# A four-layer graph network on one core: the row gathers written out without index copies and bounds, the attention sums' one-hots moved from VectorE to ScalarE

## The chip, the cores and the metric

The kernel runs on one core of one Trainium2 chip. The metric is the time of one execution on the device in microseconds. The kernel before was timed twice: 10643.65 and 10651.53 us, median 10647.59 us.

## What is computed

A graph of 6250 nodes (256 features each) and 100,000 edges, which are sorted by their destination. Each of four layers normalizes the node rows (layernorm, then max with 0), runs a graph layer over the edges and adds the result to the node rows:

```
edge_index = jnp.stack([src, dst])
h = jnp.maximum(_layernorm(x), 0.0); x = x + _L0_gnn_ref(h, ...)    # attention, 4 heads, feed-forward, 2 batch norms
h = jnp.maximum(_layernorm(x), 0.0); x = x + _L1_gnn_ref(h, ...)    # weighted sums over edges, both directions
h = jnp.maximum(_layernorm(x), 0.0); x = x + _L2_gnn_ref(h, ...)    # two rounds of plain sums: segment_sum(h[src], dst)
h = jnp.maximum(_layernorm(x), 0.0); x = x + _L3_gnn_ref(h, ...)    # attention, 8 heads
```

In layer 0 the weight of an edge is `exp(att . leaky(xl[src] + xr[dst]))` over its sum by destination, in layer 3 it comes from `s_u[src] + s_v[dst]` in the same way. What all layers share is the gather of table rows by `src` and the sum of edge rows by `dst` (`segment_sum`).

## The kernel before

**Edges as tiles.** The edges are padded to 784 tiles of 128 edges, one edge to a partition. Two tiles are a pair (392 pairs), 128 nodes are a node tile (49). A visit is a pair of edge tiles that meets one node tile: there are 440 visits, so 880 steps (one edge tile in one visit). A unit is four visits, so eight steps: there are 110 units. For every step the setup has put the position of each edge's destination inside the node tile into a column of `rel`, and the source node of every edge into `gidx`, one column for each edge tile.

**A sum by destination** is a matmul: for each step a 128x128 one-hot matrix (`iota == rel` column, edge on the partition, node on the free axis) is the stationary side and the edge rows are the moving side; TensorE adds the two steps of a visit up in a PSUM bank (four banks), and VectorE adds the bank to the node tile in SBUF (`add_visits`, line 956).

**A gather** is an indirect DMA that GpSimd issues (`gather`, line 1005): one for each edge tile, 128 rows of 256 to 264 floats by the 128 indices of one column. Five passes make 784 of them each:

- `attention_fetch0` (layer 0), into `regionB`: the gathered row and the destination's row (by matmul) are added, leaked (line 1378), transposed and multiplied by the attention vector, and the gathered rows are stored in DRAM (`Eb`) in the order of the edges
- `plain_pass` 'l1' (layer 1), into `rows_in`: weighted one-hots tile by tile (line 944), sums by destination, and a fold of sums of the other direction (line 1174)
- `plain_pass` 'l2a' and 'l2b' (layer 2), into `rows_in`: plain one-hots, one instruction for the eight steps of a unit (`one_hots`, line 941)
- `attention_fetch3` (layer 3), into `regionC`: the scores of the edges are added up and the rows are stored in `Eb`

The slots of the gathered rows are a ring of groups (four gathers to a group, in `attention_fetch3` eight). SyncE counts a group as landed and gives its slot back when the visits that read it are done (`landed_groups`, line 967). GpSimd's own loop is: wait for the slot (line 1010), copy the index columns of the next groups from `gidx` to a small tile `gather_rows` (`index_columns`, line 1000; four columns at a time in `attention_fetch0`, else eight) and wait for that copy (line 1002), then four or eight gathers (line 1014) with a bounds check against the table's last row. The loop's body is written out for one turn of the ring or two (48 to 32 gathers) and run over and over.

**The attention sums** (`attention_sum`, line 1405, for layer 0 as 'a0' and for layer 3 as 'a3') read the edge rows back from `Eb` in a plain DMA. For each unit VectorE does, in this order: the eight one-hots in one instruction (line 941), four multiplications of a pair's rows by their weights (line 1498), and then the four additions to the node tiles of the unit before (line 956). ScalarE waits until VectorE has done with the slot (`slot_kept`, line 1440) and copies the columns beside the 256 features (line 1444): logits, and in 'a0' also peaks and last marks, so 12 copies for a unit in 'a0' and 4 in 'a3'. TensorE (line 1466) waits for the one-hots, for ScalarE's columns (`lhs_full`), for each multiplication, and for the addition that frees its bank.

All waits are semaphores written out by hand; each engine's order of work is the order of its code. No planner is in between.

## Time and profile before

| | |
|---|---|
| time, 2 runs | 10643.65 to 10651.53 us, median 10647.59 |
| span of the profiled execution | 10655.6 us |
| TensorE matmul busy | 6231.9 us (58%) |
| VectorE busy | 5016.8 us (47%) |
| GpSimd busy | 5743.0 us (54%) |
| ScalarE busy | 1330.7 us (12%) |
| mean granted TensorE clock | 0.738 of full speed |
| bytes moved by DMA | 1358.92 MB, mean 128 GB/s |

The profile holds one execution: for each instruction its engine, start, duration and what it waited for. No time of that execution is given beside its span, which is 8 us above the median of the two runs (0.08%). The page's sum of shares is an average over stages that have different limits: GpSimd is busy in the five gather passes and idle in the attention sums, VectorE the other way round. So the rows below are taken stage by stage.

### The profile page before, as it was taken

Reading aid. Unit: us, or ns where it says so; the run is one execution under the profiler, and the core shown is the slowest. Engines: PE = TensorE matmul, PEld = TensorE weight load, DVE = VectorE, ACT = ScalarE, POOL = GpSimd, SP = SyncE. Lnnn points to the kernel's source line nnn. Section 1 sums busy time; section 2 is a strip of 40 time slices with the busy share of each in tenths; the row PEclk is TensorE's granted clock in tenths of the full one; section 3 lists DMA queues with packets and bytes.
Section 4 is the critical chain, followed back from the end, with each engine's and each line's share of the span. In section 5 each row is a group of like instructions: output and inputs, shape, how many; then the busy total and the mean of one; then the engine's idle time right before and its main releaser. Section 6 shows DMA issues by size and latency. Waiting matters only on the chain. (4 is left out here: it accounts for less than half of the span.)

```text
span 10655.6 us, 136733 instructions
## 1 busy us (share of the span) xinstructions
PE 6231.9 (58%) x24674; PEld 4869.8 (46%) x24675; DVE 5016.8 (47%) x12212; ACT 1330.7 (12%) x3940; POOL 5743.0 (54%) x5511
## 2 busy tenths in 40 slices
PE   4888975766466666555554665656665633222575
PEld 2888864545344444433333444444444433222454
DVE  6555558885444444355553222342222411115888
ACT  2122211213222222200001000010000300000000
POOL 3777740000188888866665777747776156762000
PEclk9898888888777777766666777777777655555798
DMA  4666665541277777744443333323332256662454
GB/s 147 188 189 188 187 214 167 168 148 43 57 104 105 104 105 104 99 137 136 133 129 93 88 88 89 88 79 88 88 87 85 69 178 199 198 191 85 134 169 154
DMA packets 835067, 1358.92 MB, mean 128 GB/s; under 512 B 112278, under 2 KB 488660, under 8 KB 834980
## 3 DMA queue, kind: packets, MB, share of 16 engines
q0 software_dynamic: 315328, 634.04, 27.0%
q1 hardware_dynamic: 385684, 562.46, 16.2%
q10 hardware_dynamic: 133968, 161.50, 4.9%
q8 instruction: 26, 0.43, 0.0%
q14 instruction: 61, 0.50, 0.0%
HBM read 943.05 MB, written 414.50 MB: 127 GB/s over the span
## 5 line engine op out<-in xcount | busy, mean ns | idle before, releaser
L1014 POOL DMA_INDIRECT rows_in<-table,gather_rows x2352 | 2470.6, 1050 | 944.0 <-issue 693.5
L1105 PE MATMUL ps_p<-rows_in,hot 128*128 x5280 | 1916.0, 524 | 1518.2 <-issue 527.6
L1105 PEld LDWEIGHTS ps_p<-rows_in,hot 128*128 128x128 f32 x5280 | 1312.6, 262 | 2081.5 <-issue 1850.3
L1724 POOL DMA_INDIRECT scatter_sums<-regionC,idx x880 | 1386.4, 1575 | 305.7 <-issue 245.1
L956 DVE TENSOR_TENSOR regionC<-regionC,ps_p 128x257 f32 (+2 forms) x1320 | 558.9, 423 | 1566.4 <-DVEq L953 1080.8
L1466 PE MATMUL ps_p<-regionA 128*128 128x265 f32 (+1 forms) x3520 | 964.9, 433 | 432.6 <-DVE regionB L956 199.3
L1466 PEld LDWEIGHTS ps_p<-regionA 128*128 128x128 f32 x3520 | 732.5, 213 | 664.6 <-DVE regionB L956 244.8
L1014 POOL DMA_INDIRECT regionB<-table,gather_rows x784 | 846.1, 1079 | 344.5 <-issue 293.9
L1014 POOL DMA_INDIRECT regionC<-table,gather_rows x784 | 813.0, 1037 | 297.3 <-issue 265.4
L1929 PE MATMUL psS<-dst_scores,regionA 128*128 x1760 | 393.3, 362 | 852.1 <-issue 427.1
L1929 PEld LDWEIGHTS psS<-dst_scores,regionA 128*128 128x128 f32 x1760 | 383.5, 330 | 861.9 <-issue 861.9
L1797 PE MATMUL psC<-regionC 128*128 128x128 f32 x1760 | 370.4, 377 | 653.6 <-PEq L1795 652.1
L1809 PE MATMUL psO<-regionA,regionC 128*128 x1760 | 666.0, 546 | 9.8 <-PEq L1808 2.8
L1797 PEld LDWEIGHTS psC<-regionC 128*128 128x128 f32 x1760 | 318.7, 271 | 757.9 <-issue 757.9
L956 DVE TENSOR_TENSOR regionB<-regionB,ps_p 128x265 f32 (+1 forms) x880 | 373.2, 424 | 506.3 <-DVEq L953 264.0
L1539 POOL MEMSET ones<- 128x128 f32 x2 | 0.4, 204 | 1122.8 <-POOLq L2054 954.3
L1319 PEld LDWEIGHTS psL<-att_cols,featT 128*128 128x128 f32 x3520 | 519.8, 213 | 61.9 <-issue 31.2
L1498 DVE TENSOR_TENSOR regionA<-regionA,logits 128x512 f32<-128x512 f32 x880 | 547.9, 685 | 0.0
L1809 PEld LDWEIGHTS psO<-regionA,regionC 128*128 128x128 f32 x1760 | 488.9, 292 | 119.5 <-issue 24.5
L1294 PE MATMUL psX<-regionA,regionB 128*128 x1760 | 526.6, 428 | 26.8 <-PEq L1290 20.5
L1371 DVE TENSOR_TENSOR feat<-regionB,psX 128x512 f32<-128x512 f32 x440 | 302.1, 687 | 507.2 <-DVEq L1370 357.7
L1319 PE MATMUL psL<-att_cols,featT 128*128 128x4 f32 x3520 | 471.4, 257 | 16.6 <-PEq L1312 8.3
(303 smaller groups left out, 7671.2 us busy)
## 6 DMA issues: line engine op xcount, KB each, us to landing
regionA<-edge_rows SPq DMA_DIRECT2D x880, 256.0 KB, 3.3
edge_rows<-regionB SPq DMA_DIRECT2D x196, 512.0 KB
edge_rows<-regionC SPq DMA_DIRECT2D x392, 256.0 KB
regionC<-srcrow_d SPq DMA_DIRECT2D x220, 256.0 KB
scatter_sums<-zero_rows ACTq DMA_DIRECT2D x8, 6400.0 KB, 42.2
regionA<-scatter_sums ACTq DMA_DIRECT2D x49, 1024.0 KB
rows_in<-table,gather_rows POOLq DMA_INDIRECT x2352
regionB<-rrow_d ACTq DMA_DIRECT2D x110, 256.0 KB
```

Source lines behind the costliest of these rows:

```text
L956: v.tensor_tensor(dst_, dst_, ps[(u.c * VG + j) % nbank][:, 0:width], ALU.add).then_inc(s_add.sem, 1)
L1014: g.indirect_dma_start(out=rows_of(b * per + j), out_offset=None, in_=table, in_offset=bass.IndirectOffsetOnAxis(ap=rows[j], axis=0), boun ...
L1105: x = te.matmul(ps[(u.c * VG + j) % NB][:, 0:width], hot[:, b, 2 * j + k, :], at_tile(G, slot[j] * 2 + k), start=k == 0, stop=k == 1)
L1294: x = te.matmul(psX[b][:, k * D:(k + 1) * D], spread[:, ub, at:at + P], at_tile(A256, nt), start=True, stop=True)
L1319: x = te.matmul(psL[gb][:, col:col + HEADS0], featT[:, b, 2 * k + c, :], attc[:, c, :], start=c == 0, stop=c == 1)
L1371: v.tensor_tensor(feat[:, b, :], G[:, bass.ds(slot * 2, 2), :].rearrange('p a c -> p (a c)'), psX[b][:, :], ALU.add).then_inc(own_v, 1)
L1466: x = te.matmul(ps[(u.c * VG + j) % NB][:, 0:width], hot[:, b, 2 * j + k, :], Gs[:, b * GS + 2 * j + k, :], start=k == 0, stop=k == 1)
L1498: v.tensor_tensor(o, i, w, ALU.mult).then_inc(aux_full[b], 1)
L1724: g.indirect_dma_start(out=scat, out_offset=bass.IndirectOffsetOnAxis(ap=idx[:, b, j:j + 1], axis=0), in_=sums[:, b, j, :], in_offset=None ...
L1797: x = te.matmul(psC[b][:, j * P:(j + 1) * P], hot[:, b * Q + j, :], same[:, b * Q + j, :], start=True, stop=True)
L1809: x = te.matmul(psO[2 * b + j // 2][:, j % 2 * D:(j % 2 + 1) * D], pairs[:, b * Q + j, :], at_tile(SUP, nt[j // 2]), start=True, stop=True)
L1929: x = te.matmul(psS[b][:, j * HEADS3:(j + 1) * HEADS3], spread[:, b, j * P:(j + 1) * P], at_tile(SV, nt[j // 2]), start=True, stop=True)
```

## The change

Three things, and small ones beside them:

- `gather` has no loop any more: all 784 gathers of a pass are written out, each with its own fixed column of `gidx` as the index, so that the copy to `gather_rows` and the wait for it are gone, and the bounds check too.
- In `attention_sum` VectorE no longer makes the one-hots. ScalarE does, after its wait for the slot and before its copies: eight activations `Square(iota - rel)` of 128x128 with a column of `minus` (= -rel) as bias, a wait for them, and one `Relu(1 - x)` over the 128x1024 of the unit. Peaks and last marks lie in one table of five columns, so that 'a0' has 8 copies for a unit instead of 12.
- In 'l2a' and 'l2b' the plain one-hots are made by eight `tensor_scalar` of 128x128 instead of one `tensor_tensor` of 128x1024.
- Beside these: the group number in the waits of TensorE (line 1102) and VectorE (line 1368) is masked with 255, and SyncE reads one number with `value_load`.

```
@@ -909,13 +909,13 @@
                         v.sem_inc(res_free[b], 1)
-                    if last is not None:
+                    if peak is not None:
                         for c in range(SB):
                             v.sem_inc(res_full[b], -1)
-                            v.tensor_copy(peak[:, c * P:(c + 1) * P, :], ps[b][:, 0:512].rearrange('p (h s) -> p s h', s=P))
-                            v.tensor_copy(last[:, c * P:(c + 1) * P], psE[b][:, 0:P]).then_inc(own_v, 1)
+                            v.tensor_copy(peak[:, c * P:(c + 1) * P, 0:H], ps[b][:, 0:512].rearrange('p (h s) -> p s h', s=P))
+                            v.tensor_copy(peak[:, c * P:(c + 1) * P, H], psE[b][:, 0:P]).then_inc(own_v, 1)
                             v.wait_ge(own_v, 1)
@@ -936,9 +936,8 @@
                     x.then_inc(hot_full[0], 1)
-def one_hots(v, hot, u):
-    shape = [P, GS, P]
-    return v.tensor_tensor(hot, iota[:, :].unsqueeze(1).to_broadcast(shape), rel[:, bass.ds(u.val * GS, GS)].unsqueeze(2).to_broadcast(shape), ALU.is_equal)
+def one_hot(v, hot, s):
+    return v.tensor_scalar(hot, iota[:, :], rel[:, bass.ds(s, 1)], None, ALU.is_equal)
 def weighted_one_hot(v, hot, s, wgt):
@@ -966,7 +965,6 @@
     behind = ring // 2
-    regs = registers(sp, 'by_visit', 1)
     def group(u):
@@ -977,7 +975,7 @@
         b = u.c % ring
-        done = of_visits(sp, visits_by[0:1, :], u.val, regs, NV)[0]
+        done = sp.value_load(visits_by[0:1, bass.ds(u.val, 1)], min_val=1, max_val=NV)
         if kept:
@@ -993,34 +991,20 @@
         sp.sem_inc(ring_free[b], -1)
-def index_columns(g, u, ring, per, idx, together):
-    b, at = (u.c % (together * ring), u.c % together)
-    if at == 0:
-        n = together * per if not isinstance(u.val, int) else min(together * per, ET - u.val * per)
-        g.tensor_copy(idx[:, b * per:b * per + n], gidx[:, bass.ds(u.val * per, n)]).then_inc(own_p, 1)
-        g.wait_ge(own_p, 1)
-        g.sem_inc(own_p, -1)
-    return [idx[:, b * per + j:b * per + j + 1] for j in range(per)]
-
-def gather(g, table, rows_of, s_rows, ring, per, free, idx, together):
-    top_row = g.to_reg(NP - 1)
-
-    def fetch(u):
-        b = u.c % ring
+def gather(g, table, rows_of, s_rows, ring, per, free):
+    for n in range(ET // per):
+        b = n % ring
         g.wait_ge(free[b], 1)
         g.sem_inc(free[b], -1)
-        rows = index_columns(g, u, ring, per, idx, together)
         for j in range(per):
-            g.indirect_dma_start(out=rows_of(b * per + j), out_offset=None, in_=table, in_offset=bass.IndirectOffsetOnAxis(ap=rows[j], axis=0), bounds_check=top_row, oob_is_err=True).then_inc(s_rows[b].sem, 16)
-    for t_ in turns(g, ET // per, together * ring, 0):
-        fetch(t_.at(0))
+            column = n * per + j
+            g.indirect_dma_start(out=rows_of(b * per + j), out_offset=None, in_=table, in_offset=bass.IndirectOffsetOnAxis(ap=gidx[:, column:column + 1], axis=0)).then_inc(s_rows[b].sem, 16)
 def plain_pass(name, table, acc, acc_flat, width, weighted, fold=None, own=None):
         G = sb('rows_in', [P, RG * EG, width], F32, ctx)
-        idx = sb('gather_rows', [P, 2 * RG * EG], I32, ctx)
         hot = sb('hot', [P, 2, GS, P], F32, ctx)
@@ -1086,7 +1070,7 @@
             def _(g):
-                gather(g, table, lambda k: G[:, k, 0:D], s_rows, RG, EG, ring_free, idx, 2)
+                gather(g, table, lambda k: G[:, k, 0:D], s_rows, RG, EG, ring_free)
             @block.tensor
@@ -1099,7 +1083,7 @@
                     for j in range(VG):
-                        te.wait_ge(s_landed.sem, group[j] + s_landed.base)
+                        te.wait_ge(s_landed.sem, (group[j] & 255) + s_landed.base)
                         te.wait_ge(s_add.sem, u.val * VG + (j + 1) + s_add.base)
@@ -1155,7 +1139,8 @@
                     else:
-                        x = one_hots(v, hot[:, b], u)
+                        for j in range(GS):
+                            x = one_hot(v, hot[:, b, j, :], u.val * GS + j)
                     x.then_inc(hot_full[b], 1)
@@ -1255,7 +1239,7 @@
             def _(g):
-                gather(g, T0, lambda k: G[:, k, :], s_rows, RG0, EG, ring_free, idx, 1)
+                gather(g, T0, lambda k: G[:, k, :], s_rows, RG0, EG, ring_free)
             @block.scalar
@@ -1365,7 +1349,7 @@
                     group = v.snap(groups[u.c % VG], min_val=0, max_val=NEG)
-                    v.wait_ge(s_landed.sem, group + s_landed.base)
+                    v.wait_ge(s_landed.sem, (group & 255) + s_landed.base)
                     v.wait_ge(res_full[b], 1)
@@ -1412,6 +1396,7 @@
     with ExitStack() as ctx:
+        minus = sb('minus_rel', [P, S], F32, ctx)
         ps = [bank(f'ps_p{i}', ctx) for i in range(NB)]
@@ -1438,6 +1423,12 @@
                     a.sem_inc(slot_kept[b], -1)
+                    for j in range(GS):
+                        x = a.activation(hot[:, b, j, :], iota[:, :], ACT.Square, bias=minus[:, bass.ds(u.val * GS + j, 1)])
+                    x.then_inc(own_a, 1)
+                    a.wait_ge(own_a, 1)
+                    a.sem_inc(own_a, -1)
+                    a.activation(hot[:, b].rearrange('p s e -> p (s e)'), hot[:, b].rearrange('p s e -> p (s e)'), ACT.Relu, bias=1.0, scale=-1.0).then_inc(hot_full[b], 1)
                     for j in range(VG):
@@ -1474,6 +1465,9 @@
                     v.sem_inc(back_free[b], 1)
+                v.tensor_scalar(minus[:, :], rel[:, :], -1.0, None, ALU.mult).then_inc(own_v, 1)
+                v.wait_ge(own_v, 1)
+                v.sem_inc(own_v, -1)
                 for b in (0, 1):
@@ -1481,7 +1475,6 @@
                     pair = of_visits(v, pair_of, u.val * VG, pairs, PAIRS - 1)
-                    one_hots(v, hot[:, b], u).then_inc(hot_full[b], 1)
                     v.wait_ge(s_back_in[lb], 16 * VG)
@@ -1901,7 +1893,7 @@
             def _(g):
-                gather(g, T4, lambda k: G[:, k, :], s_rows, R3, GS, free3, idx, 1)
+                gather(g, T4, lambda k: G[:, k, :], s_rows, R3, GS, free3)
             @block.scalar
@@ -2042,12 +2034,11 @@
     attention_fetch0(LG, attc, B)
-    PK = sb('peaks', [P, SP_, HEADS0], F32, L0)
-    LS = sb('last_marks', [P, SP_], F32, L0)
-    segment_softmax(LG, LG[:, :, :], HEADS0, (A, B), last=LS[:, :], peak=PK, by_step=True, beside=lambda a: zero_sums(a, range(3, CHAINS)))
+    PK = sb('peaks_last', [P, SP_, HEADS0 + 1], F32, L0)
+    segment_softmax(LG, LG[:, :, :], HEADS0, (A, B), peak=PK, by_step=True, beside=lambda a: zero_sums(a, range(3, CHAINS)))
     WB = D + 2 * HEADS0 + 1
     ACCB = tiles(B, WB)
-    attention_sum('a0', LG, HEADS0, True, [(PK, HEADS0), (LS[:, :].unsqueeze(2), 1)], ACCB, B[:, 0:NT * WB], A)
+    attention_sum('a0', LG, HEADS0, True, [(PK, HEADS0 + 1)], ACCB, B[:, 0:NT * WB], A)
     with ExitStack() as ctx:
```

## Rows read from the trace of the kernel before

**Rows 1.** Busy time by stage: fetch0, a0, l1, l2a, fetch3, a3; columns in the header.

```profile
...
core 0: us, PE busy (x) PEld busy (x) DVE busy (x) ACT busy (x) POOL busy (x), PEclk, DMA share, GB/s
262.20:1504.90 1242.70, 1106.54 (x6864) 1008.64 (x6863) 663.50 (x1074) 253.74 (x428) 897.60 (x979) 0.88 0.61 188
1679.00:2391.00 712.00, 481.57 (x1760) 364.07 (x1760) 600.29 (x1021) 142.96 (x1300) 0.00 (x0) 0.90 0.51 161
4536.90:5729.60 1192.70, 628.55 (x1748) 441.99 (x1748) 634.84 (x1409) 0.00 (x0) 817.29 (x881) 0.68 0.43 129
5793.60:6958.20 1164.60, 704.86 (x2044) 493.77 (x2044) 342.90 (x598) 38.58 (x97) 864.21 (x881) 0.73 0.31 88
...
8463.50:9686.00 1222.50, 386.14 (x1728) 376.54 (x1728) 203.60 (x719) 0.00 (x0) 833.00 (x881) 0.50 0.66 193
9905.00:10610.00 705.00, 489.67 (x1787) 372.77 (x1785) 594.22 (x998) 61.93 (x440) 0.00 (x0) 0.89 0.52 164
...
```

**Rows 2.** Groups of GpSimd, stage by stage in that order: busy, mean ns, idle before.

```profile
...
L1014 POOL DMA_INDIRECT regionB<-table,gather_rows x784 | 846.1, 1079 | 344.5 <-issue 293.9 <-POOLq L1002 31.8 <-POOL gather_rows L1000 11.9
...
L1000 POOL COPY gather_rows<-gidx 128x4 int32 x191 | 50.8, 266 | 1.2
...
L1014 POOL DMA_INDIRECT rows_in<-table,gather_rows x784 | 798.0, 1018 | 346.4 <-issue 232.4 <-POOLq L1011 67.8 <-POOL gather_rows L1000 26.2
...
L1014 POOL DMA_INDIRECT rows_in<-table,gather_rows x784 | 836.5, 1067 | 297.4 <-issue 229.9 <-POOL gather_rows L1000 25.4 <-POOLq L1002 21.4
...
L1014 POOL DMA_INDIRECT regionC<-table,gather_rows x784 | 813.0, 1037 | 297.3 <-issue 265.4 <-POOL gather_rows L1000 16.8 <-POOLq L1002 14.4
...
```

**Rows 3.** Timeline in l2a: start, duration (us), idle before in brackets.

```profile
...
6302.02 1.01 POOL L1014 DMA_INDIRECT rows_in<-table,gather_rows  x1 [0.30 <-issue]
6303.03 0.19 POOL L1000 COPY gather_rows<-gidx 128x8 int32 x1
6304.02 1.04 POOL L1014 DMA_INDIRECT rows_in<-table,gather_rows  x1 [0.79 <-POOLq L1002]
...
6309.22 1.22 DVE L941 TENSOR_TENSOR hot<-iota,rel 128x1024 f32<-128x1024 f32 x1
6309.31 2.02 POOL L1014 DMA_INDIRECT rows_in<-table,gather_rows  x1 [0.30 <-issue]
...
```

**Rows 4.** Timeline in l2a: the first gather after the loop jumps back.

```profile
...
5961.47 1.01 POOL L1014 DMA_INDIRECT rows_in<-table,gather_rows  x1 [1.77 <-issue]
...
```

**Rows 5.** Timeline of VectorE in fetch0 after its last gather has landed.

```profile
...
1520.28 0.69 DVE L1371 TENSOR_TENSOR feat<-regionB,psX 128x512 f32<-128x512 f32 x1 [0.17 <-DVEq L1370]
...
1522.42 0.69 DVE L1371 TENSOR_TENSOR feat<-regionB,psX 128x512 f32<-128x512 f32 x1 [0.52 <-DVEq L1370]
...
```

**Rows 6.** Timeline of one unit of the attention sum a3.

```profile
...
10203.72 0.56 ACT L1444 ACTIVATE regionA<-logits 128x16 f32 x4 [5.57 <-ACTq L1440]
...
10204.34 1.22 DVE L941 TENSOR_TENSOR regionA<-iota,rel 128x1024 f32<-128x1024 f32 x1 [0.44 <-issue]
10205.49 2.49 DVE L1498 TENSOR_TENSOR regionA<-regionA,logits 128x512 f32<-128x512 f32 x4
10207.89 0.42 DVE L956 TENSOR_TENSOR regionC<-regionC,ps_p 128x264 f32 x1
...
10208.37 5.35 PE L1466 MATMUL ps_p<-regionA 128*128 128x264 f32 x16 [2.31 <-DVE regionC L956]
...
10210.48 1.23 DVE L941 TENSOR_TENSOR regionA<-iota,rel 128x1024 f32<-128x1024 f32 x1 [0.44 <-issue]
...
```

**Rows 7.** Groups of ScalarE and VectorE that price the new one-hots: busy, mean ns.

```profile
...
L944 DVE TENSOR_SCALAR hot<-iota,rel,step_weights 128x128 f32<-128x128 f32 x880 | 250.8, 363 | 123.2 <-issue 71.0 <-DVEq L1146 38.7 <-DVEq L1185 7.0
...
L1842 DVE TENSOR_SCALAR regionC<-regionC 128x128 f32<-128x128 f32 x880 | 202.0, 298 | 0.0
...
L1594 ACT ACTIVATE squares<-regionC 128x1792 f32 (+1 forms) x14 | 23.8, 1700 | 91.8 <-ACTq L1593 91.8
...
L936 ACT ACTIVATE regionA<-regionA 128x896 f32<-128x896 f32 x12 | 11.4, 950 | 133.1 <-ACTq L935 133.0
...
```

**Rows 8.** Timeline of ScalarE: two activations of 128x128 with a bias column.

```profile
...
2551.92 0.62 ACT L520 ACTIVATE mid_T<-psM,mid_bias 128x128 f32<-128x128 f32 x2 [0.51 <-ACTq L518]
...
```

More of the change, by code:

```diff
@@ L665, in kchunks, with segment_softmax @@
             return w.rearrange('(k p) n -> p k n', p=P)
-        def segment_softmax(LG, logits, heads, room, last=None, peak=None, beside=None, by_step=False):
+        def segment_softmax(LG, logits, heads, room, peak=None, beside=None, by_step=False):
             H = 4
@@ L911, in _ @@
                                 v.sem_inc(res_free[b], 1)
-                            if last is not None:
+                            if peak is not None:
                                 for c in range(SB):
```

4 lines of the change are left out of this document (1 added, 3 removed).

## The prediction

> **What bounds the kernel now.** The page's totals (GpSimd 54%, TensorE 58%, VectorE 47%) name no limit, so I first cut the span into stages with the busy-time table [rows 1]. In the gather passes GpSimd is busy 817 to 898 us of 1165 to 1243, and TensorE is close to it only in fetch0 (1106.5 of 1242.7). In the two sums VectorE is busy 600.3 of 712 and 594.2 of 705 us, and GpSimd does nothing.
>
> Second view, the groups of GpSimd by stage [rows 2]: are its idle times waits, or its own gaps? In l2a the 784 gathers are busy 836.5 us and idle 297.4 us before them, the copies take most of the rest of the 1164.6. Of the 297.4, 686 x 0.30 + 98 x 0.79 = 283 us are the fixed gaps that the timeline shows [rows 3]: 0.30 us between two gathers, 0.79 between an index copy and the gather behind it. So l2a, and l2b like it (1168 us), is bound by the issue of gathers, at 1164.6 / 784 = 1.49 us each where a bare gather costs 1.01 + 0.30 = 1.31. Fetch0 copies every four gathers and runs at 1.59. In l1 67.8 us and in fetch3 1222.5 - 833.0 - 297.3 = 92 us are real waits for a free slot; the rest is issue there too.
>
> Third, the timeline of a unit in a3 [rows 6]: VectorE has one gap of 0.44 us in the 6.14 us from one block of one-hots (10204.34) to the next (10210.48). It is the bound. ScalarE works 0.56 us of it, and TensorE waits 2.31 us for VectorE. 110 units of 6.14 make 675 of the 705 us; a0 is alike.
>
> **Part 1, gathers without copy and loop.** For each copy GpSimd loses its 0.19 us and 0.79 - 0.30 = 0.49 us [rows 3], and a jump of the loop costs 1.77 - 0.30 = 1.47 us [rows 4], some 8 times in a pass. New cost of a pass is busy time of its gathers + 784 x 0.30 = 235 us + the waits that remain:
> - fetch0: 846.1 + 235 = 1081 us, 161 less. Once the last gather has landed, its visits go through at 1522.42 - 1520.28 = 2.14 us each [rows 5], 440 of them 942 us, so the rest of the pass can follow 1081. But TensorE is busy 1106.5 us at a granted clock of 0.88 [rows 1], so I take off a little: 140.
> - l1: 798 + 235 + 79 of waits (the 29 before copies, and of the 346.4 what the fixed gaps and jumps leave) = 1112 us, 80 less. A faster GpSimd meets the full ring more often: I take 50.
> - fetch3: 813 + 235 + 92 = 1140 us, 82 less. It waits for slots already: 60.
> - l2a and l2b: 836.5 + 235 = 1072 us, 93 less each, before part 2.
>
> SyncE's queue gets nothing new, and its reading of one number by another call is one for one. The gathers move the same bytes, earlier: the DMA share goes from 0.61 to about 0.7 in fetch0 and from 0.66 to 0.7 in fetch3, below what would queue them. The mask with 255 is one register operation for a visit on TensorE's and VectorE's sequencers, which wait for gathers there: nothing, and if that cover were gone at most 1760 times 0.11 us, the pace of ScalarE's copies with their register arithmetic (143.0 / 1300 in a0) [rows 1], 194 us. The bounds check has no price in the trace: every gather has one. The nearest rows are a gather's 1.01 us itself, and no reason is seen why it should cost more without. I take 0, and for the low end of the range 0.1 us of each of 3920.
>
> **Part 2, plain one-hots tile by tile (l2a, l2b).** On VectorE eight plain `tensor_scalar` cost 8 x 202.0 / 880 = 1.84 us [rows 7] in place of 1.22, so 68 us more in a pass on an engine that is busy 343 of 1165 [rows 1]: hidden, and 136 us for both passes if it weren't. Off VectorE it does more. A gather that starts beside the 1.22 us instruction takes 2.02 us instead of 1.01 [rows 3], and the mean of a gather is 1067 ns in l2a but 1018 ns in l1, whose one-hots are eight `tensor_scalar` already [rows 2, 7]. So 784 x 0.049 = 38 us go as well: 93 + 38 = 131 us for each pass. With a little for new waits: 115 each, 230 for both.
>
> Here a rule speaks against the change. By the Trainium skill (SBUF — State Buffer, "Who interferes with whom") a `tensor_scalar` that runs in a two-port mode keeps GpSimd out completely while it runs, and `tensor_tensor` with two SBUF inputs only bars its reads. The trace of l1 doesn't show it: by that rule the passes would lose time, which is rival 4.
>
> **Part 3, one-hots to ScalarE (a0, a3).** VectorE loses the 10205.49 - 10204.34 = 1.15 us of each unit [rows 6]. What ran beneath it comes out: the wait for the rows and the address arithmetic of the first multiplication, between 0 and the 0.44 us of the gap already there; I take 0.25. VectorE's unit is then 5.24 us. Can ScalarE follow? Its eight squares start 0.62 - 0.36 = 0.26 us apart [rows 8], 7 x 0.26 + 0.36 = 2.2 us; the Relu over 1024 columns lies between the 950 ns of 896 and the 1700 of 1792 [rows 7], 1.06 us; the wait between them at most 0.3 (the gap of rows 3); the copies are 143.0 / 110 x 8/12 = 0.87 us in a0 and 0.56 in a3 [rows 1]. That is 4.4 and 4.1 us, below 5.24. What is late next is TensorE's start. ScalarE begins when VectorE has released the slot, about 10203.9 in the rows, and TensorE started 4.5 us later; without the one-hots it could start 3.6 later, and now waits for ScalarE's 4.4. Its products are wanted only in the next unit's additions, and its busy time is 481.6 / 110 = 4.4 us of 5.24 [rows 1], but a unit at reduced clock takes 5.35 [rows 6], over the new unit. So I take 0.8 us of the 0.9: 220 x 0.8 = 176 us. Ends: 0, if ScalarE needed 6.14 us, and 220 x 1.15 = 253. The plain read of `Eb` rises from a DMA share of 0.52 to 0.62 and still lands in time. Four copies fewer in a0 count in ScalarE's sum above; `minus` is one instruction for each sum, under 1 us.
>
> **The sum.** 140 + 50 + 60 + 230 + 176 = 656 us. The span of 10655.6 becomes 10000; it stands 8 us over the median of the runs, so the time is 10647.6 - 656 = 9992 us.
>
> **Rivals.**
> 1. *The next bound takes over at once.* TensorE in fetch0 (clock 0.88, busy 89%), the full ring in l1 and fetch3, and TensorE at clock 0.73 in l2 let only half of each pass's gain through: 240 + 176 = 416, 10,232 us. For it: the waits of 68 and 92 us. Against: in l2a almost none.
> 2. *ScalarE becomes the bound of the sums.* Eight squares with a register-made bias column at 0.5 us each would make its unit 6.2 us, and part 3 gives nothing: 10,168 us. Against: its copies, with register arithmetic for each, come 0.11 us apart.
> 3. *A gather without bounds check is quicker*, by 0.1 us: 78 us more in l2a, l2b, and with what rings and TensorE let through some 250 in all: 9742 us. Nothing shows it, nothing excludes it.
> 4. *VectorE's small instructions shut GpSimd out.* 110 units x 1.84 us = 202 us in each l2 pass: 798 + 235 + 202 = 1235 instead of 1165, so +70 in place of -115, twice: 656 - 370 = 286 saved, 10,362 us. Against: l1's 1018 ns.
> 5. *Slower: written-out gathers run out of code.* 4800 instructions replace loops of 32 to 48 gathers. Where code isn't at hand a gather comes 1.47 us late [rows 4]; if each of the 980 groups of four paid that, 1440 us would come on top: 11,432 us. It decides against the change from (656 + 213) / 980 = 0.89 us for a group. The jump is the only such delay seen. The Trainium skill (Runtime: NRT & Kernel Launch, "Instruction fetch mechanics") holds that straight code is fetched ahead and that a taken branch is what stalls, which speaks against this rival; no run here shows long straight code on GpSimd yet.
>
> **How the numbers follow.** Forecast 0.50, rival 1 0.14, rival 2 0.10, rival 3 0.14, rival 4 0.05, rival 5 0.04, and 0.03 for a mixture that cancels. The forecast's own range is 9890 to 10,110. The range of 8 in 10 reaches to rivals 1, 2 and 3: 9740 to 10,260. Within 2% is about what a measurement of this kernel can't tell from no change; all but the last two cases are faster by more: 0.93, same 0.03, slower 0.04.
>
> **What would show it.** Part 1: no copies on GpSimd, gathers 1.31 us apart, stages of about 1100, 1140, 1050, 1050 and 1160 us; a gap other than 0.30 or a busy time other than 1.01 shows rival 5 or 3. Part 2: the mean gather in l2a near 1018 ns; over 1100 is rival 4. Part 3: units of 5.3 us, the largest wait of TensorE no longer VectorE but ScalarE; VectorE idle before its additions would be rival 2. The prediction is wrong if GpSimd waits for slots over 100 us in l2a, or if the sums stay above 680 us.

## The result: slower by 2.4%, where faster was forecast

| | before | changed |
|---|---|---|
| median of 2 runs | 10647.59 us | 10905.62 us (10896.9 to 10914.34) |
| ratio, 95% | | 1.0237 [1.0207, 1.0267] |
| span of the profiled execution | 10655.6 us | 10895.1 us |
| GpSimd busy | 5743.0 us | 5234.5 us |
| mean granted TensorE clock | 0.738 | 0.726 |

Two later runs of the changed kernel beside the kernel before gave 1.0205 [1.0176, 1.0234] and 1.0221 [1.0204, 1.0238]. The forecast was 9992 us. One of the ten executions of the changed kernel (in x15_changed_again) took 21,061 us at a granted clock of 1.0; it has no trace, is left out of the medians and stays unexplained.

Busy time by stage in the changed kernel, against [rows 1] (window, its length, busy us and instructions of PE, PEld, DVE, ACT and POOL, then clock, DMA share, GB/s). The windows are fetch0, l1, l2a, l2b and fetch3 from first to last gather:

```profile
261.00:1738.80 1477.80, 1217.07 (x6768) 1098.09 (x6769) 655.13 (x1059) 248.00 (x422) 779.07 (x784) 0.79 0.50 157
...
4677.40:5887.20 1209.80, 604.70 (x1728) 426.73 (x1728) 631.21 (x1398) 0.00 (x0) 745.66 (x784) 0.69 0.42 127
5953.60:7175.80 1222.20, 639.70 (x2031) 460.05 (x2030) 393.96 (x1359) 38.58 (x97) 744.06 (x784) 0.69 0.29 84
7289.20:8507.40 1218.20, 649.00 (x2022) 459.89 (x2020) 391.69 (x1351) 38.56 (x97) 743.66 (x784) 0.69 0.29 84
8736.80:10024.90 1288.10, 386.14 (x1728) 376.55 (x1728) 204.32 (x719) 0.00 (x0) 756.15 (x784) 0.50 0.61 183
```

GpSimd has 72 to 120 us less to do in each pass than in [rows 1], and every pass is longer: fetch0 by 235 us, l1 by 17, l2a by 58, l2b by 50, fetch3 by 66. The sums are shorter: from the first addition to the last, a0 takes 570 us (before 677), and a3 ends 99 us nearer to fetch3. That makes 206 us, where part 3 was forecast at 176.

Where the time in the passes goes, the groups of the whole changed kernel say, against [rows 2]:

```profile
L1001 POOL DMA_INDIRECT rows_in<-table,gidx x2352 | 2233.5, 950 | 1609.8 <-POOLq L998 946.3 <-issue 642.8 <-SPq L982 15.0
...
L1001 POOL DMA_INDIRECT regionB<-table,gidx x784 | 779.1, 994 | 705.7 <-POOLq L998 486.9 <-issue 216.2 <-SPq L982 2.6
L1001 POOL DMA_INDIRECT regionC<-table,gidx x784 | 756.2, 965 | 761.3 <-POOLq L998 526.5 <-issue 230.2 <-SPq L1881 4.6
```

L998 is GpSimd's wait for a free slot of the ring. Without the waits for the stages before, it comes to 487, 243, 268, 257 and 297 us in the five passes, where it was 7, 96, 24, 29 and 90. The gather itself became quicker, 950 to 994 ns for 1018 to 1079. So GpSimd no longer sets the time of the passes. The engines that read the rows do, and they are slower than GpSimd was. SyncE's waits in fetch0 say the same (line waited for, releaser, us in total, times, longest):

```profile
SPq L982 <- DVEq L1361: 985.6, 168, 13.2
SPq L1234 <- DMA regionB<-table,gidx: 10.7, 2, 7.0
```

It waited 278.0 us for gathers there before the change, and 5.2 us for visits to be done.

Two places show the readers. At the start of fetch0 (timeline: start, duration, idle before) VectorE stands still for 29 us while GpSimd issues gathers 1.25 us apart, and goes on some 7 us after the ring is full and GpSimd stops:

```profile
281.10 0.95 POOL L1001 DMA_INDIRECT regionB<-table,gidx  x1 [0.30 <-POOLq L998]
282.35 0.95 POOL L1001 DMA_INDIRECT regionB<-table,gidx  x1 [0.30 <-issue]
...
287.53 0.69 DVE L1362 SCALAR_TENSOR_TENSOR feat<-feat 128x512 f32<-128x512 f32 x1 [0.24 <-DVE feat L1355]
...
309.83 0.95 POOL L1001 DMA_INDIRECT regionB<-table,gidx  x1 [0.30 <-issue]
...
317.50 0.69 DVE L1355 TENSOR_TENSOR feat<-regionB,psX 128x512 f32<-128x512 f32 x1 [29.27 <-DVEq L1354]
...
320.73 1.13 POOL L1001 DMA_INDIRECT regionB<-table,gidx  x1 [9.95 <-POOLq L998]
```

In l2a, TensorE's matmuls come 1.5 to 5 us apart in one unit, again beside gathers 1.25 us apart. Of its waits there, 4.29 and 0.78 us have no releaser ("issue"), and 3.66 us go to VectorE's addition, which itself came late:

```profile
6346.18 0.67 PE L1089 MATMUL ps_p<-rows_in,hot 128*128 x2 [4.29 <-issue]
...
6347.63 1.22 PE L1089 MATMUL ps_p<-rows_in,hot 128*128 x2 [0.78 <-issue]
...
6350.86 0.95 POOL L1001 DMA_INDIRECT rows_in<-table,gidx  x1 [0.30 <-issue]
...
6352.11 0.95 POOL L1001 DMA_INDIRECT rows_in<-table,gidx  x1 [0.30 <-issue]
...
6352.51 1.20 PE L1089 MATMUL ps_p<-rows_in,hot 128*128 x2 [3.66 <-DVE regionC L955]
```

A unit of a3, against [rows 6], is as forecast: 5.14 us from the first addition of a unit to that of the next, and ScalarE's squares and Relu lie beside VectorE's work:

```profile
10311.37 0.42 DVE L955 TENSOR_TENSOR regionC<-regionC,ps_p 128x264 f32 x1
...
10313.34 2.45 ACT L1427 ACTIVATE regionA<-iota,minus_rel 128x128 f32<-128x128 f32 x8 [1.09 <-ACTq L1425]
10314.09 2.50 DVE L1491 TENSOR_TENSOR regionA<-regionA,logits 128x512 f32<-128x512 f32 x4 [0.58 <-DVEq L1479]
10315.92 1.06 ACT L1431 ACTIVATE regionA<-regionA 128x1024 f32<-128x1024 f32 x1
10316.51 0.42 DVE L955 TENSOR_TENSOR regionC<-regionC,ps_p 128x264 f32 x1
```

### The profile page after: what moved, and what is told of

It reads as the page before. It is cut to its first block and busy times, and to the rows that moved or that the text cites. A ratio compares the mean times of both kernels' runs of the same rounds, so it can differ in the third digit from the quotient of the medians.

```text
span 10895.1 us, 143605 instructions
## 1 busy us (share of the span) xinstructions
PE 6105.6 (56%) x24674; PEld 4815.5 (44%) x24675; DVE 4880.9 (45%) x13534; ACT 2026.5 (19%) x5480; POOL 5234.5 (48%) x4923
## 5 line engine op out<-in xcount | busy, mean ns | idle before, releaser
L1001 POOL DMA_INDIRECT rows_in<-table,gidx x2352 | 2233.5, 950 | 1609.8 <-POOLq L998 946.3
L1089 PE MATMUL ps_p<-rows_in,hot 128*128 x5280 | 1802.0, 499 | 1753.3 <-issue 1202.9
L1089 PEld LDWEIGHTS ps_p<-rows_in,hot 128*128 128x128 f32 x5280 | 1250.5, 250 | 2266.7 <-issue 2075.6
L1001 POOL DMA_INDIRECT regionC<-table,gidx x784 | 756.2, 965 | 761.3 <-POOLq L998 526.5
L1001 POOL DMA_INDIRECT regionB<-table,gidx x784 | 779.1, 994 | 705.7 <-POOLq L998 486.9
L1457 PE MATMUL ps_p<-regionA 128*128 128x265 f32 (+1 forms) x3520 | 855.0, 396 | 334.3 <-PEq L1452 213.5
L1457 PEld LDWEIGHTS ps_p<-regionA 128*128 128x128 f32 x3520 | 659.5, 192 | 529.5 <-DVE regionB L955 192.7
L1303 PEld LDWEIGHTS psL<-att_cols,featT 128*128 128x128 f32 x3520 | 570.6, 233 | 213.0 <-issue 177.4
L1278 PE MATMUL psX<-regionA,regionB 128*128 x1760 | 584.1, 465 | 22.7 <-PEq L1274 16.4
L1427 ACT ACTIVATE regionA<-iota,minus_rel 128x128 f32<-128x128 f32 x1760 | 538.2, 388 | 274.5 <-ACTq L1425 274.5
```

Of the source, the lines that this page charges most:

```text
L1001: g.indirect_dma_start(out=rows_of(b * per + j), out_offset=None, in_=table, in_offset=bass.IndirectOffsetOnAxis(ap=gidx[:, column:column ...
L1089: x = te.matmul(ps[(u.c * VG + j) % NB][:, 0:width], hot[:, b, 2 * j + k, :], at_tile(G, slot[j] * 2 + k), start=k == 0, stop=k == 1)
L1278: x = te.matmul(psX[b][:, k * D:(k + 1) * D], spread[:, ub, at:at + P], at_tile(A256, nt), start=True, stop=True)
L1303: x = te.matmul(psL[gb][:, col:col + HEADS0], featT[:, b, 2 * k + c, :], attc[:, c, :], start=c == 0, stop=c == 1)
L1427: x = a.activation(hot[:, b, j, :], iota[:, :], ACT.Square, bias=minus[:, bass.ds(u.val * GS + j, 1)])
L1457: x = te.matmul(ps[(u.c * VG + j) % NB][:, 0:width], hot[:, b, 2 * j + k, :], Gs[:, b * GS + 2 * j + k, :], start=k == 0, stop=k == 1)
```

## The experiments

Ratios are to the kernel before, timed beside it. In most experiments that kernel took 10,641 to 10,673 us. Beside x12_stream_a3, x13_paused_a3 and x14_mixed_pace it took 10,463 us; they are marked "quick chip" here, and the expectations call it the other chip. That it was another chip is not shown: the record numbers the chip of those three 0, and that of x16_changed_third and x17_stream_a3_again, beside which the kernel before took 10,662 us, 0 as well.

### First four: which part

**x1_loop**: the gathers of before in the changed kernel.

```diff
-            for n in range(ET // per):
+            for t_ in turns(g, ET // per, together * ring, 0):   # index_columns and bounds_check back
```

> The changed kernel with GpSimd's gathers as they were before: looped code, an index copy for every four or eight, bounds check. The masks, the asserted read of one number on SyncE, the small one-hots and part 3 stay. Theory A (written-out gather code on GpSimd starves the other engines' sequencers of code: in l2a TensorE's matmuls of one visit come 4 to 5 us apart after its loop's jump while gathers run at 1.25 us): the five passes return to about their spans before (1243, 1193, 1165, 1168, 1223 us), the 206 us of part 3 stay, and the time is about 10,440 us. Theory B (the added register instructions on SyncE and TensorE make their loop bodies too long to be at hand): passes stay near 1210 to 1290 us and the time is at 10,850 or above, since the copies come on top. Theory C (the quicker gathers without bounds check fill the ring and nothing else matters): about 10,440 too, so A and C are told apart by the run with the bounds check.

Measured: 10506.51 us, 0.9871 [0.9855, 0.9888]. Fetch0, l1 and fetch3 are back at 1241, 1189 and 1219 us; l2a and l2b, with part 2 still in, take 1193 and 1191 us, some 25 more than before.

**x2_bounds**: `bounds_check=top_row, oob_is_err=True` back on the written-out gathers, no copies.

> The changed kernel with the bounds check back on its written-out gathers. Theory A (written-out code starves the other sequencers): no gain, 10,880 to 10,950 us, fetch0 still about 1480 us, only the mean gather goes back from 950 to some 1010 ns. Theory C (gathers without bounds check are the harm): fetch0 back to about 1250 us and the time near 10,500. Theory B (added register instructions): no change, as A.

Measured: 10853.75 us, 1.0215 [1.0188, 1.0242]; fetch0 1446 us. The ratio is not told apart from that of the changed kernel. The bounds check is the only difference: the mean gather takes 1015 to 1058 ns in the five passes, 64 to 68 ns more than without.

**x3_loop_wide**: as x1_loop, and part 2 undone.

```diff
-                                for j in range(GS):
-                                    x = one_hot(v, hot[:, b, j, :], u.val * GS + j)
+                                x = one_hots(v, hot[:, b], u)
```

> As the run with looped gathers, and with the plain one-hots of l2a and l2b as one instruction for eight steps again (part 2 undone). My step on part 2 had 38 us for a pass, 76 for both: then this is 76 us slower than the run with looped gathers alone. If VectorE's small instructions held GpSimd up (rival 4) it is faster by as much as 140. Theory A or B make no difference between the two.

Measured: 10469.23 us, 0.9842 [0.9825, 0.9858]: 37 us faster than x1_loop. Part 2 costs time.

**x4_masks**: the kernel before with `(group & 255)` on TensorE and VectorE and `value_load` on SyncE.

> The kernel before with nothing but the register instructions of the change: the count of a group masked with 255 ahead of each wait on TensorE and VectorE, and SyncE's number read with an assertion of its bounds. Theory B: this alone makes the three plain passes 20 to 60 us longer each and fetch0 longer by up to 235, so 10,780 to 11,000 us. Theory A: within 0.3% of before, 10,620 to 10,680 us. My prediction priced it at 0, with 194 us as its bound.

Measured: 10670.47 us, 1.0027 [1.0016, 1.0038]: 29 us, not the bound of 194. x3_loop_wide is this kernel with part 3, so part 3 is worth 10670.5 - 10469.2 = 201 us.

At this point I took written-out code for the harm. The next four refuted that.

### Second four: what of the gathers

**x5_straight_copies**: x3_loop_wide with the gather loop written out.

```diff
-            for t_ in turns(g, ET // per, together * ring, 0):
+            for t_ in turns(g, ET // per, ET, 0):
```

> The kernel of the run with looped gathers and wide one-hots (10,469 us), with one edit: the gathers' loop is written out for all 196 (98) groups; index copies and bounds check stay. If the straight code itself is the harm, fetch0 takes 1400 us or more although its gathers keep their old pace, fetch3 1250 or more, and the time is 10,700 to 10,900 us. If the harm needs the faster pace (a full ring behind which SyncE's two jobs block each other), the passes keep their 1242 to 1190 us less the jumps' 12 us, and the time is about 10,420.

Measured: 10446.13 us, 0.9805 [0.9789, 0.9822], with x7_turns the fastest version. Straight code does no harm.

**x6_loop_nobounds**: x3_loop_wide without bounds check.

> The same looped kernel (10,469 us) without the bounds check of its gathers, loop and copies kept. From the changed kernel's mean gather of 950 ns against some 1010 with the check: 3920 x 0.06 = 235 us less GpSimd time, of which the passes bound by issue (l2a, l2b, fetch0) should give back about 0.06 x 784 = 47 us each: about 10,250 to 10,330 us if only straight code is harmful. If faster gathers are what hurts, fetch0 grows instead, over 1300 us, and the time is 10,500 or more.

Measured: 10722.34 us, 1.0056 [1.0037, 1.0076]: by the ratios 230 us slower than x3_loop_wide, for quicker gathers (980 ns for 1079 in fetch0); fetch0 takes 1415 us. Its index copies, and so its pauses, are those of before.

**x7_turns**: x3_loop_wide with longer loop bodies.

> The same looped kernel (10,469 us) with longer loop bodies, another one for each pass: 128 gathers in fetch0 (before 32), 96 in l1, 192 in l2a, 96 in fetch3 (before 48), and l2b written out. If code that was run a moment ago is still at hand up to some length, the passes under that length keep their time and those over it look like written-out code: l2b is then the longest against its 1173 us, as TensorE's first matmuls after its jumps come late; the pass with 192 gathers shows whether that length is passed. If the length of GpSimd's code is of no account all passes stay within 10 us of 1242, 1188, 1171, 1173 and 1232 us.

Measured: 10440.8 us, 0.9799 [0.9782, 0.9815]; passes of 1241, 1198, 1174, 1175 and 1227 us. The length of GpSimd's code is of no account.

**x8_scalar_stream**: written-out work on ScalarE in l1.

> The same looped kernel (10,469 us); only in l1 ScalarE, which has nothing there but 49 transfers to start, runs a written-out stream of 3136 copies of 8 columns into a spare tile (additional work; its result is not used). If any engine's straight code takes the code supply from the others, l1 grows from 1188 us to 1210 or more and its matmuls wait longer with no releaser named; if the harm is GpSimd's own (its indirect transfers), l1 stays at 1188 and the time at 10,470.

Measured: 10470.91 us, 0.9829 [0.9813, 0.9846]. l1 took 1211 us, over the mark of 1210 that was set for a harm, against 1188 in x3_loop_wide and 1198 in x7_turns: a harm of 13 to 23 us at most, and none in the whole time.

### Third: the pace

**x9_pace_memset**: the changed kernel, in fetch0 and fetch3 with

```diff
+                    if room is not None and j % 4 == 3:
+                        g.wait_ge(own_p, 1)
+                        g.sem_inc(own_p, -1)
+                        g.memset(room[:, :], 0.0).then_inc(own_p, 1)   # room: 128 x 1500
```

> The changed kernel (written out, no copies, no bounds check), and in fetch0 and fetch3 alone GpSimd clears 1500 columns of a spare tile behind every fourth gather (additional work, some 1.3 us, so a gather every 1.58 us as before the change, with the gaps of 0.30 us kept). So far: written-out code is harmless (10,446 us), a loop without bounds check is slow (10,722). Theory C (a gather every 1.25 to 1.48 us is more than the consumers take, the ring fills, and a pass with a full ring goes slower than one that is paced): fetch0 back from 1478 to about 1250 us, fetch3 from 1288 to about 1230, the time about 10,620. Theory D (what helps is not the pace but GpSimd's pauses of 0.79 us): fetch0 stays at 1400 us or more and the time above 10,850.

Measured: 10612.92 us, 0.9966 [0.9951, 0.9981]. More work on GpSimd made the kernel 290 us faster; fetch0 fell from 1478 to 1274 us. GpSimd is busy with the clearing in that time, so what helps the others is that no gather is being issued, not that GpSimd rests.

**x10_pause_by_two**: the changed kernel, 8 columns cleared and waited for behind every second gather.

> The changed kernel, and behind every second gather of all five passes GpSimd clears 8 columns of a spare tile and waits for it (additional work, about 0.2 + 0.49 us, so a gather every 1.59 us with a pause in each pair). Theory C: fetch0 about 1250, the plain passes about 784 x 1.59 = 1247 us since they are bound by that pace, fetch3 about 1250; the time about 10,650. Theory D: the pauses let the other sequencers go on: the same in fetch0. This run and the one with the long clearing tell C and D apart together: both short is C, this alone is D; both long in fetch0 speaks against both.

Measured: 10782.02 us, 1.0124 [1.0105, 1.0142]; fetch0 1314, plain passes 1253 to 1255, fetch3 1271 us.

**x11_fetch0_by_two**: x5_straight_copies with eight gathers for a copy in fetch0, not four.

> The written-out kernel with copies and bounds check (10,446 us), and in fetch0 one index copy for eight gathers in place of four, so a gather every 1.50 us in place of 1.585. Theory C: this is near where the consumers' own pace lies (the loop without bounds check, at 1.48, fell to 1415 us for the pass): either the pass gains at most 784 x 0.085 = 67 us (10,380) or, if the ring fills, it takes over 1350 and the time is 10,550 or more. My prediction's arithmetic, in which each faster gather shortens the pass, says 10,380.

Measured: 10612.37 us, 0.9962 [0.9946, 0.9979]; fetch0 1402 us. 98 copies fewer made fetch0 160 us longer, where the prediction's arithmetic said 67 us shorter.

Fetch0 in these kernels. The interval from one gather to the next is worked out: the mean gather, a gap of 0.30 us, and what is put in, divided by the gathers between (0.68 us for a copy, 0.66 for a small clearing with its wait, and for the long one its 1.37 us less the 0.14 by which the gap behind it is shorter).

| kernel | interval of issue, us | fetch0, us | TensorE busy x clock |
|---|---|---|---|
| changed | 1.29 | 1478 | 1217 x 0.79 |
| x2_bounds | 1.36 | 1446 | 1197 x 0.80 |
| x11_fetch0_by_two | 1.44 | 1402 | 1187 x 0.80 |
| x6_loop_nobounds | 1.45 | 1415 | 1218 x 0.79 |
| x5_straight_copies | 1.55 | 1242 | 1103 x 0.88 |
| x9_pace_memset | 1.62 | 1274 | 1110 x 0.89 |
| x10_pause_by_two | 1.66 | 1314 | 1153 x 0.84 |

Between 1.45 and 1.55 the pass falls by 160 to 173 us. In the last three rows it is GpSimd's own time within 27 us (784 times the interval is 1215, 1270 and 1301 us); in the first four it is 273 to 467 us longer than that. The interval orders these rows better than the pauses do: x6_loop_nobounds and x5_straight_copies have the same index copies and the same pauses of 0.79 us behind them, and differ by 173 us. The rows of x11_fetch0_by_two, x6_loop_nobounds, x5_straight_copies and x9_pace_memset:

```profile
262.70:1664.90 1402.20, 1186.93 (x6746) 1067.98 (x6745) 652.05 (x1056) 249.32 (x422) 869.66 (x881) 0.80 0.52 165
```

```profile
261.80:1676.50 1414.70, 1217.88 (x6759) 1091.27 (x6759) 653.93 (x1059) 250.00 (x423) 836.92 (x979) 0.79 0.51 164
```

```profile
261.70:1503.50 1241.80, 1102.77 (x6834) 1001.13 (x6834) 661.53 (x1070) 252.97 (x427) 896.98 (x979) 0.88 0.60 188
```

```profile
262.70:1537.00 1274.30, 1110.25 (x6962) 1015.59 (x6963) 686.72 (x1089) 256.86 (x435) 1063.50 (x979) 0.89 0.59 183
```

The product of busy time and clock is 950 to 988 in all seven: about the same work, at a lower clock where TensorE's work is broken up.

**x14_mixed_pace** (quick chip): no bounds check but in fetch0, a copy for every four gathers in l1, l2a and fetch3, for eight in l2b.

> The written-out kernel with copies (10,446 us), gathers without bounds check in l1, l2a, l2b and fetch3 and with it in fetch0; an index copy for every four gathers in l1, l2a, fetch3 (a gather every 1.25 + 0.17 = 1.42 us with a pause after four), for every eight in l2b (1.34). Before, these passes are issued at 1.49 us. If short pauses are enough for the others, l1, l2a and fetch3 gain up to 0.07 x 784 = 50 us each (10,300); if a pass with a full ring always loses, they stay or grow: l2a 1185, l2b 1190 us or more as in the loop without bounds check, and the time is 10,450 to 10,520.

Measured: 10274.19 us, 0.9818 [0.9801, 0.9834], beside a kernel before of 10463.19 us. Against x12_stream_a3 (the kernel of x5_straight_copies in these passes, quick chip too) l2b took 1103.5 us for 1160.7, but l1 1134 for 1115, l2a 1186 for 1159 and fetch3 1168 for 1141. The prediction's arithmetic of GpSimd's own time gives all four: the gathers are 49 to 77 ns quicker, and in l1, l2a and fetch3 98 more index copies cost 67 us. In l2a that is 784 x 0.052 = 41 us off and 67 on, 26 in all, and 27 were measured; in l2b, with no more copies, 60 off, and 57 were measured. Where nothing holds the readers up, part 1 of the prediction is sound.

### Last: gathers with nobody waiting for them

**x12_stream_a3** (quick chip): x5_straight_copies, and GpSimd, idle in a3, issues 440 more gathers.

```diff
+                            for n in range(N3):                     # 440
+                                if n >= 4:
+                                    g.wait_ge(spare_in[n % 4].sem, spare_in[n % 4].base + 16 * (n // 4))
+                                g.indirect_dma_start(out=spare[:, n % 4, :], ..., in_offset=...gidx[:, n:n + 1]...)
```

> The written-out kernel with copies and bounds check (10,446 us); in the attention sum a3, where GpSimd has nothing to do, it issues 440 additional gathers of 8 columns into a spare tile, one behind the other (0.30 us gaps, no pause; little data, no ring, nobody waits for them). Theory E (issuing gathers without a pause holds the other engines up, whatever the ring does): a unit of a3 goes from 5.2 us to 6 us or more while the stream runs, the sum is 50 us or more longer, with waits of VectorE and TensorE that no releaser explains. Theory F (only the full ring, by its order of waits, costs time): a3 is unchanged within 10 us.

**x13_paused_a3** (quick chip): with a pause behind every second.

> As the run with the additional stream in a3, with a pause behind every second gather (8 columns cleared and waited for, some 0.7 us). Theory E: the pauses let the others go on, so a3's loss is less than half of the unpaused stream's for each gather. If the loss of a gather is the same, the pauses do nothing and density is no part of it.

Measured: 10255.96 us, 0.9801 [0.9781, 0.9821], and 10380.82 us, 0.9920 [0.9900, 0.9940]; a3's additions take 570.3 and 570.4 us. The second is longer in all because its stream outlasts the sum. Here the stream harms nobody.

**x17_stream_a3_again**, the kernel of x12_stream_a3, now beside a kernel before of 10,662 us:

> The kernel with 440 additional gathers of 8 columns in a3, unpaused, again. On the chip where nothing holds TensorE up it changed a3 by nothing (570.3 us from the first to the last addition, 570.4 with pauses). On a chip with 10,640 to 10,670 us for the kernel before, theory E (unpaused gathers hold the other engines up there) expects a3 over 600 us and units of more than 5.5 us while the stream runs; theory F expects 570 again.

Measured: 11005.58 us, 1.0326 [1.0305, 1.0346], 560 us over x5_straight_copies; a3's additions take 1096 us for 569. Timeline of a3 with the stream:

```profile
9999.95 0.43 DVE L956 TENSOR_TENSOR regionC<-regionC,ps_p 128x264 f32 x1 [10.06 <-DVEq L953]
10000.43 0.94 POOL L1468 DMA_INDIRECT spare_rows<-table,gidx  x1 [0.30 <-issue]
...
10001.68 0.94 POOL L1468 DMA_INDIRECT spare_rows<-table,gidx  x1 [0.30 <-issue]
...
10011.85 0.43 DVE L956 TENSOR_TENSOR regionC<-regionC,ps_p 128x264 f32 x1 [11.47 <-remote]
10012.11 2.44 ACT L1448 ACTIVATE regionA<-iota,minus_rel 128x128 f32<-128x128 f32 x8 [40.74 <-issue]
```

One addition in 12 us, where a unit with its four takes 5.2; 53 of the 440 additions fall into the 570 us. The stretch of the stream, and the same kernel's on the quick chip (x12_stream_a3):

```profile
9862.00:10432.00 570.00, 111.70 (x221) 62.48 (x220) 56.06 (x106) 51.02 (x169) 436.26 (x423) 0.51 0.14 29
```

```profile
9639.00:10180.00 541.00, 395.73 (x1659) 306.31 (x1658) 428.31 (x828) 404.61 (x1341) 412.56 (x422) 1.00 0.67 205
```

**x18_paused_a3_again**, with the pauses, beside a kernel before of 10,648 us:

> The kernel with 440 additional gathers in a3 and a pause behind every second one, again. The unpaused stream just took 11,006 us on a chip of the usual kind, 560 us more than the kernel without it, with 10 to 12 us from one addition of VectorE to the next; on the other chip neither stream changed a3. If pauses let the other engines go on (theory E with D's pauses), a3 takes 570 to 640 us from its first addition to its last and the time is about 10,560 or less; if only the number of gathers counts, a3 again takes 1100 us and the time is about 11,000.

Measured: 10561.24 us, 0.9919 [0.9890, 0.9948]. The stream lasts 704 us, beyond the end of the sum, and the sum runs as if it were not there:

```profile
9829.00:10370.00 541.00, 396.88 (x1661) 307.14 (x1661) 426.96 (x827) 404.82 (x1341) 353.08 (x503) 1.00 0.66 204
```

**x15_changed_again** and **x16_changed_third**, the changed kernel itself, were to meet the quick chip and did not (the kernel before took 10,673 and 10,662 us):

> The changed kernel itself once more. The last three runs shared a chip on which the kernel before takes 10,463 us in place of 10,641 to 10,657 us, and on which TensorE's four matmuls of a visit in fetch0 end after 1.15 us at full clock whatever GpSimd does, where they took 2.0 to 4.9 us beside two to four gathers in the profile of the changed kernel. Theory G (the loss belongs to chips on which gathers hold TensorE and the sequencers up): if this run's kernel before takes about 10,463 us, the changed kernel is faster there, by my sum about 10,463 - 600 = 9,860 us, and its TensorE shows 1.15 us; if it takes about 10,650 us, the ratio is again about 1.02. Theory F (a full ring costs time by its order of waits, on any chip): 1.01 to 1.03 on either.

> The changed kernel a third time, to see it beside a kernel before of about 10,463 us if this chip is one of that kind. Theory G: about 9,860 us there, with fetch0 at 1080 to 1120 us; on a chip with 10,640 to 10,670 us the ratio is 1.02 again. Theory F: 1.01 to 1.03 on either.

Measured: 10901.56 and 10891.67 us, 1.0205 and 1.0221. What the changed kernel does beside a kernel before of 10,463 us stays open.

## Why the prediction was wrong

**The step that failed** is in part 1: "its visits go through at 1522.42 - 1520.28 = 2.14 us each [rows 5], 440 of them 942 us, so the rest of the pass can follow 1081". The 2.14 us were read where GpSimd had stopped; in the changed kernel a visit takes 1477.8 / 440 = 3.36 us. I took the readers' speed to be independent of the gathers; it is not. For each visit of fetch0 this is the time from TensorE's first weight load of `psX` to the event of the semaphore that this visit raises for VectorE (the ends of matmuls on the page are modelled, this event is recorded), at full clock, by the number of gathers started from 4 us before its last weight load to 0.5 us after (mean us, visits):

```
gathers in those 4.5 us     0          1          2           3           4
before                                            2.38 (77)   3.08 (267)  2.87 (8)
changed                     1.15 (6)   1.17 (22)  2.67 (75)   4.46 (132)  6.18 (46)
x12 (quick chip)                       1.15 (1)   1.16 (102)  1.16 (243)  1.15 (13)
```

Four matmuls, the same data: 1.15 us alone, 6.18 beside four gathers (one visit of 40 us among them; the median is 5.8). The "2.0 to 4.9 us" in the expectation of x15_changed_again are too low: they took the first event of either of two semaphores, at times that of the visit before. The kernel before, too, paid for its gathers, but its copies made a pause of 0.98 us behind every fourth or eighth [rows 3]. The change took the pauses away and made the gathers quicker, and the readers lost more than GpSimd gained. x17 and x18 show this without a ring and without a reader: 440 gathers in a row make the sum 527 us longer, the same gathers with 0.90 us in place of 0.30 behind every second leave it as it is. Whether the pauses count or the lower rate that they make (1.60 us a gather for 1.25), no run tells apart; in fetch0 the pauses alone were not enough (x6_loop_nobounds).

Two things are late. The first is TensorE's signal that its matmuls are done: from the start of a visit's last matmul in a3 to its semaphore the median is 9.0 us in the stretch of the stream (x17_stream_a3_again, 55 visits) and 0.4 us in x5_straight_copies, x12_stream_a3 and x18_paused_a3_again. In fetch0 the mean is 2.72 us in the changed kernel, 2.10 before and 0.44 in x12_stream_a3. Whether the matmuls themselves ran late or only the signal, the trace does not tell.

The second is the sequencers' own work, in some of the stages. A register operation of TensorE's queue ahead of the wait for a group, in l1, l2a and l2b (minimum, median, longest ns), in the changed kernel and in x10_pause_by_two:

```profile
L1086 PEldq ALU_OP  x2640: 2/36/1422, 4679.4 to 8516.5; - x189
```

```profile
L1091 PEldq ALU_OP  x2640: 36/36/36, 4488.5 to 8429.8; - x189
```

It works on a register alone, and yet takes up to 1.4 us beside unpaused gathers; with a pause in every pair, never more than 36 ns. This is not the measure of the loss. In fetch0, which lost most, no such operation of TensorE's or VectorE's queue took over 101 ns; there it is SyncE's instructions that take up to 1.4 us. And x5_straight_copies, the fastest version, has 259 of 4141 such operations of TensorE's queue over 0.3 us in these three passes (changed 667 of 4127, before 31 of 2822). That the code of the others arrives late would explain the second and not the first; it was only argued, and why gathers hold the others up stays open.

**Point by point.**

- *Part 1, some -410 of the sum's 480 for parts 1 and 2*: measured +390, from the ratio of x1_loop against that of the changed kernel (0.0366 x 10,647 us). The arithmetic of GpSimd's own time was right: without copies, 1.25 to 1.29 us a gather, which is 1.31 less the quicker gather; x14_mixed_pace bears it out. It stopped being the bound.
- *The bounds check at 0*: wrong. Without it the gather takes 949 to 994 ns, 0.06 to 0.07 us less in the pair that differs in nothing else (the changed kernel against x2_bounds), and 0.06 to 0.10 in x6_loop_nobounds against x3_loop_wide; rival 3 said 0.1. But in this last pair, with the copies kept, the quicker gather cost 230 us. Rival 3 had the right fact and the wrong sign.
- *Part 2, -76 us*: half right. The mean gather in l2a fell from 1062 to 1020 ns (x3_loop_wide to x1_loop), where 1018 was forecast. The pass grew from 1171 to 1193 us, and TensorE's clock in it fell from 0.73 to 0.67. +37 us for both passes.
- *Part 3, -176 us*: right, 201 us (x3_loop_wide against x4_masks), with a unit of 5.14 to 5.2 us where 5.24 was said. ScalarE did not become the bound.
- *"SyncE's queue gets nothing new", the mask at nothing*: both not so. SyncE's queue has 784 new assertion instructions, one for each group that it gives back, and TensorE's and VectorE's have the masks. Together they cost 29 us (x4_masks), inside the bound of 194. That is their price at the old rate of gathers: every kernel with faster gathers has them too, so what they cost beside those is not shown and lies within the 390 us.
- *Rival 1*, the next bound, took over, but at more than the old time; by halving the gains it left that out. *Rival 4*: VectorE's small one-hots did not slow the gathers (1020 ns). *Rival 5*, slower by running out of code, had the sign and not the cause: with copies and bounds check the written-out gathers are 23 us faster than the loop (x5_straight_copies against x3_loop_wide), and their gaps are the 0.30 and 0.79 us of the loop. The rule I cited against it, that straight code is fetched ahead (the Trainium skill, Runtime: NRT & Kernel Launch, "Instruction fetch mechanics"), these numbers of x5_straight_copies bear out.
- *What would prove it wrong* was named: over 100 us of slot waits in l2a. There were 333.8 - 66.3 (the wait ahead of the stage) = 268 us.

The sum: 390 + 37 + 29 - 201 = 255 us; the changed kernel is 258 us slower. The four terms are steps of one chain of kernels from the changed one to the one before, so that the sum closes proves none of them by itself.

**Still open**: why fetch0 jumps between 1.45 and 1.55 us. TensorE's clock falls from 0.88 to 0.80 across the jump, so part of the jump may be the clock; no run sets the clock by itself. Open too is what differed on the quick chip.

**Best version**: x5_straight_copies (gathers written out, index copies and bounds check kept, one wide one-hot in l2, one-hots of the sums on ScalarE), 0.9805 [0.9789, 0.9822]: 2% under the kernel before and 4% under the changed one. x7_turns (0.9799) is not told apart from it.

## What to carry to other kernels

Read a reader's speed beside the traffic that it will have, not in the quiet tail of a pass: a wait that is taken from the bounding engine can be what lets the others work. When GpSimd issues gathers in a row, look for waits for TensorE that outlast its matmuls by microseconds, and for instructions of SyncE's queue that take 0.7 us or more; if there are some, try fewer gathers in a given time, by a pause or other work, before you try more speed. And test each part alone: the one good part here was worth 2%, hidden under two bad ones.

## What the runs showed of the hardware

- Unpaused gathers on GpSimd (0.30 us gaps) hold TensorE, VectorE, ScalarE and SyncE up, with little data moved (29 GB/s in the stretch of x17_stream_a3_again, where 53 of the 440 additions were done in 570 us). With 0.90 us behind every second gather (x18_paused_a3_again) all 440 were done in 570 us.
- TensorE's semaphore comes late beside them: a median of 9.0 us behind the start of the visit's last matmul in that stretch of x17_stream_a3_again, 0.4 us in x18_paused_a3_again and in x5_straight_copies.
- It isn't so every time, and whether that lies in the chip is not shown. Where the kernel before took 10,463 us in place of 10,641 to 10,673, the kernel with the stream took 10,256 in place of 11,006, and no register operation of TensorE's loops was late: over the whole kernel the longest of its loop counters took 36 ns there (x12_stream_a3) and 1396 ns in the slower case (x17_stream_a3_again):

```profile
L71 PEldq ALU_OP  x435: 32/36/36, 179.7 to 10195.4; - x145
```

```profile
L71 PEldq ALU_OP  x435: 5/36/1396, 179.3 to 10945.0; - x145
```

- A gather of 128 rows without bounds check takes GpSimd 0.06 to 0.07 us less (x2_bounds against the changed kernel), and up to 0.10 in x6_loop_nobounds against x3_loop_wide.
